# Last expert layer: gated expert rows added to token rows in DRAM tile by tile, then copied to the result

## What is computed

```python
    def _L1_ffn_ref(x, Wg, bg, W1, b1, W2, b2):
        ...
        logits = xf @ Wg.T + bg
        probs = jax.nn.softmax(logits, axis=-1)
        top2_vals, top2_idx = jax.lax.top_k(probs, 2)
        cw = jnp.zeros((n, Wg.shape[0]), dtype=x.dtype)
        cw = cw.at[jnp.arange(n)[:, None], top2_idx].set(top2_vals)
        h = jax.nn.gelu(jnp.einsum('nd,edh->neh', xf, W1) + b1[None], approximate=False)
        y = jnp.einsum('neh,ehd->ned', h, W2) + b2[None]
        out = jnp.einsum('ne,ned->nd', cw, y)
        return out.reshape(b, t, d)
    ...
    x = x + _L1_ffn_ref(_layernorm(x, axis=-1)[None], L1_ffn_Wg, L1_ffn_bg, L1_ffn_W1, L1_ffn_b1, L1_ffn_W2, L1_ffn_b2)[0]
    return x
```

## Time and profile before

| | us |
|---|---|
| median of three runs | 2013.77 (2011.37 to 2014.79) |
| the profiled execution | 2016.99 |
| its span in the profile | 2015.1 |

### The profile page before, as it was taken

One profiled execution on the slowest core, in us unless ns is written; L12 is line 12 of the kernel. 1 busy time (PEld: TensorE's weight loads), 2 busy tenths in 40 slices (PEclk: granted clock), 3 DMA queues, 4 the chain that ended last, 5 costly groups with the idle time before them and its releaser, 6 DMA issues.

```text
span 2015.1 us, 24539 instructions
## 1 busy us (share of the span) xinstructions
PE 1849.3 (92%) x8418; PEld 1165.9 (58%) x8419; DVE 746.1 (37%) x1688; ACT 401.5 (20%) x1065; POOL 128.5 (6%) x212
## 2 busy tenths in 40 slices
PE   7999999998899998599997999999999999599980
PEld 4555566566533344366666965555588589365650
DVE  3212222686688989511114311141111133311114
ACT  2431210024211222111102422000221211222110
POOL 0000000000000000111114100000000000111105
PEclk9999999999899999699998999999999999699995
DMA  6004000000000101545556111010010011545437
GB/s 183 0 1 165 3 1 0 20 1 1 14 35 33 44 28 42 196 142 185 190 185 169 55 47 47 0 47 0 1 47 1 0 55 47 203 141 182 177 117 229
DMA packets 58060, 153.06 MB, mean 76 GB/s; under 512 B 12526, under 2 KB 23170, under 8 KB 57525
## 3 DMA queue, kind: packets, MB, share of 16 engines
q1 hardware_dynamic: 34053, 87.05, 12.5%
q0 software_dynamic: 13120, 35.86, 5.9%
q10 hardware_dynamic: 10800, 28.98, 3.9%
HBM read 121.37 MB, written 33.99 MB: 77 GB/s over the span
## 4 chain that ended last, share of the span: by engine, by line
PE 81%; DVE 8%; DMA 5%; issue 2%; DVEq 2%; ACT 1%; POOL 1%; ACTq 0%; SPq 0%; POOLq 0%
PE PS L646 23%; PE PS L975 10%; PE PS L656 7%; PE PS L795 6%; PE PS L1016 4%; PE PS L1085 4%; PE PS L717 4%; PE PS L1105 4%; PE PS L1057 4%; DVE WRA L1727 3%; PE PS L1043 3%; PE PS L884 2%; DMA WS<-in_fW 2%; PE PS L893 2%; DVE WRB L1727 2%
## 5 line engine op out<-in xcount | busy, mean ns | idle before, releaser
L646 PE MATMUL PS<-WS,XT 128*125 128x384 f32 x960 | 313.3, 488 | 1.4 <-issue 1.4
L646 PEld LDWEIGHTS PS<-WS,XT 128*125 128x125 f32 x960 | 180.4, 189 | 129.3 <-issue 3.4
L975 PE MATMUL PS<-WS,XGT 128*128 x600 | 199.9, 491 | 0.0
L975 PEld LDWEIGHTS PS<-WS,XGT 128*128 128x128 f32 x600 | 113.2, 192 | 74.7 <-issue 2.5
L656 PE MATMUL PS<-XT,WS 128*128 128x416 f32 (+1 forms) x432 | 151.2, 512 | 0.0
L1727 DVE SCALAR_TENSOR_TENSOR WRA<-RB,U,AT 125x500 f32<-125x500 f32 (+1 forms) x240 | 140.1, 648 | 9.5 <-ACT AT L1205 6.8
L1856 DVE TENSOR_TENSOR YS<-PS,EBB 128x768 f32<-128x768 f32 x48 | 46.0, 958 | 256.9 <-PE PS L975 192.1
L656 PEld LDWEIGHTS PS<-XT,WS 128*128 128x128 f32 x432 | 81.6, 189 | 69.2 <-issue 69.2
L884 PE MATMUL PS<-WRA,F 125*64 125x500 f32 (+1 forms) x480 | 100.5, 537 | 10.1 <-DVE WRA L1727 9.5
L1085 PE MATMUL PS<-WS,XGT 128*128 x288 | 101.9, 505 | 7.6 <-DMA WS<-in_fW 4.9
L1105 PE MATMUL PS<-WS,HT 128*128 x276 | 94.5, 493 | 2.5 <-ACT HT L1414 2.5
(11 more groups left out here) (293 smaller groups left out, 2244.6 us busy)
## 6 DMA issues: line engine op xcount, KB each, us to landing
WS<-in_ewT SPq DMA_DIRECT2D x8, 2304.0 KB, 10.6
expert_rows<-YS ACTq DMA_DIRECT2D x48, 384.0 KB, 2.3
WS<-in_fW SPq DMA_DIRECT2D x16, 1152.0 KB, 7.5
WS<-in_w SPq DMA_DIRECT2D x5, 2304.0 KB, 10.4
xn_rows<-XN ACTq DMA_DIRECT2D x20, 336.0 KB
RB<-expert_rows SPq DMA_DIRECT2D x12, 488.3 KB
WS<-in_wp SPq DMA_DIRECT2D x2, 2304.0 KB, 11.5
WS<-in_W SPq DMA_DIRECT2D x2, 2304.0 KB, 8.1
```

Source lines behind the costliest of these rows:

```text
L646: last = nc.tensor.matmul(ps[0:T, 0:HC], lhsT[:, k, t * T:(t + 1) * T], w[:, k, b * HC:(b + 1) * HC], start=(k == 0), stop=(k == KC - 1))
L975: last = nc.tensor.matmul(PS[:, 4 + 2 * a + b, 0:HC], XGT[:, a, k, :], WS[:, bass.ds(slot, 1), k * C + b * HC:k * C + (b + 1) * HC].rearra ...
```

## The change

- While the last convolution is added (agg2_t), SP writes each finished tile of X to `expert_rows` in DRAM, at the token's own row: 20 DMAs.
- The gates are brought into tile order. DVE splits each gate into three bfloat16 parts and multiplies them into OT (TVG); PE multiplies this with OHR in 20 bfloat16 matmuls into a free PSUM bank; DVE sums the parts (GTE, the gate of each row of each tile) and forms SIDX, the DRAM row that each row of a tile belongs to. A padding row gets a row of its own behind the tokens.
- In the loop DVE multiplies YS by the gate after adding the bias (one more instruction a tile).
- ACT stores nothing any more. POOL issues, for each tile, an indirect DMA that adds the 128 rows of YS to their rows in DRAM. Each waits until the add of the tile before it has landed, as two tiles can hold the same token. POOL's index instructions are written in one stream: gather, add, gather, add.
- The 20 gathers, the 20 weighted sums and the 20 stores at the end are gone. When the last add has landed, SP and ACT copy one half each of the 1250 rows from `expert_rows` to the result, DRAM to DRAM.

POOL's inner loop of the last layer, half a turn of it, before. `turned_n30` counts tiles that PE has transposed, `ys_out30` and `ys_out31` the transfers out of the two YS buffers, `ys_ready` the tiles that DVE has scaled.

The diff, without the buffers' and semaphores' declarations and without the first layer, whose code is written out anew but does the same:

```diff
+            sp.wait_ge(dve_emptied, J.emptied("dve", J.at[f"agg2_{t}"] + 1))
+            sp.dma_start(y_d[t * T:t * T + PA, :], X[0:PA, t, :]).then_inc(acc_in, 16)
+            sp.dma_start(y_d[t * T + PA:(t + 1) * T, :], X[PA:T, t, :]).then_inc(acc_in, 16)
         sp.wait_ge(stage_done, 4)
         load(U_FF + 1)
...
-        for t in range(NT):
-            sp.wait_ge(yg_used[3], summed(3, 2 * t + 1))
-            sp.dma_start(out[t * T:t * T + PA, :], X[0:PA, t, :]).then_inc(stored, 16)
-            sp.dma_start(out[t * T + PA:(t + 1) * T, :], X[PA:T, t, :]).then_inc(stored, 16)
-        sp.wait_ge(stored, 32 * NT)
+        sp.wait_ge(y_all, 2)
+        sp.dma_start(out[0:N // 2, :].rearrange("n c -> (n c)").rearrange("(a b) -> a b", b=1920),
+                     y_d[0:N // 2, :].rearrange("n c -> (n c)").rearrange("(a b) -> a b", b=1920)).then_inc(stored, 16)
+        sp.wait_ge(stored, 32)
...
-        gathers(1, 1)
-        gathers(3, 2)
...
+        def add_rows(n, a, landed):
+
+
+            pool.wait_ge(ys_ready, n + 1)
+            for b, count in landed:
+                pool.wait_ge(ys_out[3][b], count * 16)
+            nc.gpsimd.sem_inc(pool_step, 1)
+            nc.gpsimd.tensor_tensor(SXF[:, a:a + 1], SIDX[:, bass.ds(n, 1)], ones[:, 0:1], ALU.mult)
+            pool.drain()
+            nc.gpsimd.tensor_copy(SX[:, a:a + 1], SXF[:, a:a + 1])
+            pool.drain()
+            nc.gpsimd.indirect_dma_start(out=y_d, out_offset=bass.IndirectOffsetOnAxis(ap=SX[:, a:a + 1], axis=0),
+                                         in_=YS[:, a, :], in_offset=None, compute_op=ALU.add).then_inc(ys_out[3][a], 16)
+
+        def gather3(n, a, turned):
+            pool.wait_ge(turned_n[3], turned)
+            nc.gpsimd.sem_inc(pool_step, 1)
+            gather(3, n, a)
+
+        first_gathers(3, 2)
+        n = nc.gpsimd.value_load(TAB[0:1, 2, 2:3], min_val=KT // 2 - 3, max_val=ET_MAX // 2 - 3)
+        over = nc.gpsimd.value_load(TAB[0:1, 2, 1:2], min_val=1, max_val=2)
+        for m in (2, 3, 4):
+            gather3(m, m % 2, m)
+        pool.wait_ge(gates_in, 1)
+        pool.wait_ge(acc_in, 32 * NT)
+        add_rows(0, 0, [])
+        with nc.gpsimd.Fori(0, n) as i:
+            gather3(i * 2 + 5, 1, i * 2 + 5)
+            add_rows(i * 2 + 1, 1, [(0, i + 1)])
+            gather3(i * 2 + 6, 0, i * 2 + 6)
+            add_rows(i * 2 + 2, 0, [(1, i + 1)])
+        gather3(n * 2 + 5, 1, n * 2 + 5)
+        add_rows(n * 2 + 1, 1, [(0, n + 1)])
+        gather3(n * 2 + 5, 0, n * 2 + 6)
+        add_rows(n * 2 + 2, 0, [(1, n + 1)])
+        add_rows(n * 2 + 3, 1, [(0, n + 2)])
+        with nc.gpsimd.Fori(0, over) as j:
+            add_rows(n * 2 + j + 4, 0, [(1, n + 2), (0, n + j + 2)])
+            gather3(n * 2 + j + 6, 0, n * 2 + j + 8)
+
+        pool.wait_ge(ys_out[3][0], (n + over) * 16 + 32)
+        pool.wait_ge(ys_out[3][1], n * 16 + 32)
+        nc.gpsimd.sem_inc(y_all, 1)
+        pool.wait_ge(xg_in[3][0], (n + over) * 16 + 64)
+        pool.wait_ge(xg_in[3][1], n * 16 + 48)
...
         turn(3, 1, 1, 16)
         hidden(0, 0)
+        pe.wait_ge(gate_parts, 1)
+        for q in range(KT):
+            last = nc.tensor.matmul(PS[:, 7, 0:4 * ETC], OHR[:, q, :], TVG[:, q, :, :].rearrange("p a b -> p (a b)"),
+                                    start=(q == 0), stop=(q == KT - 1))
+        last.then_inc(gates_full, 1)
         with nc.tensor.Fori(0, turns3) as i:
             for a in range(2):
...
             n = turns3 * 2 + j
             hidden_columns(n)
-            store(3, n, 0)
             columns_of(3, n + 1, 0, turned=n + 4, used=n + 2)
             gelu(n + 1, 0)
+        act.wait_ge(y_all, 2)
+        act.dma_start(out[N // 2:N, :].rearrange("n c -> (n c)").rearrange("(a b) -> a b", b=1920),
+                      y_d[N // 2:N, :].rearrange("n c -> (n c)").rearrange("(a b) -> a b", b=1920)).then_inc(stored, 16)
 
...
-            V.tensor_copy(IDXA, pos)
+            if L == 1:
+                V.tensor_copy(IDXA, pos)
             ps = full(J.at[f"tokens{L}"])
             step(V.tensor_scalar(TOKF, ps[:, 0:ETC], float(T), None, ALU.mult))
...
+            V.tensor_scalar(one(2)[:, 2:3], one(2)[:, 0:1], -2.0, None, ALU.add)
...
-            dve.wait_ge(ys_out[L][a], i * 16 + 16)
+            if L == 1:
+                dve.wait_ge(ys_out[L][a], i * 16 + 16)
+            elif not isinstance(i, int):
+                dve.wait_ge(ys_out[L][a], i * 16)
             V.tensor_tensor(YS[:, a, :].rearrange("p (b c) -> p b c", b=2), PS[:, b0:b0 + 2, 0:HC],
                             EBB[L][:, bass.ds(e, 1), :].rearrange("p a (b c) -> p (a b) c", b=2), ALU.add).then_inc(y_free[L], 1)
-
-        def weighted(L, t, n):
+            if L == 3:
+                V.drain()
+                V.tensor_scalar(YS[:, a, :], YS[:, a, :], GTE[:, bass.ds(n, 1)], None, ALU.mult).then_inc(ys_ready, 1)
...
+        V.drain()
+        V.tensor_copy(GPB[:, 0], GW)
+        V.drain()
+        V.tensor_tensor(GR, GW, GPB[:, 0], ALU.subtract)
+        V.drain()
+        V.tensor_copy(GPB[:, 1], GR)
+        V.drain()
+        V.tensor_tensor(GR, GR, GPB[:, 1], ALU.subtract)
+        V.drain()
+        V.tensor_copy(GPB[:, 2], GR)
+        V.drain()
+        tvg = TVG.rearrange("p (t k) v e -> p t k v e", k=2)
+        for n in range(2):
+            ot = OT.rearrange("p (t k) e -> p t k e", k=2)[:, :, n, :]
+            for m in range(3):
+                V.tensor_tensor(tvg[:, :, n, m, :], ot, GPB[:, m, n, :].unsqueeze(2).to_broadcast([T, NT, ETC]), ALU.mult)
+        V.tensor_copy(TVG[:, :, 3, :], OT)
+        V.drain().then_inc(gate_parts, 1)
         dve.wait_ge(eb_in, 48)
         turns3 = nc.vector.value_load(TAB[0:1, 2, 0:1], min_val=1, max_val=ET_MAX // 2 - 1)
         over3 = nc.vector.value_load(TAB[0:1, 2, 1:2], min_val=1, max_val=2)
...
-        with nc.vector.Fori(0, turns3) as i:
+        dve.wait_ge(gates_full, 1)
+        V.tensor_copy(GTE, PS[:, 7, 0:ETC])
+        V.tensor_scalar(SIDX, PS[:, 7, 3 * ETC:4 * ETC], -1.0, 1.0, ALU.mult, ALU.add)
+        V.tensor_scalar(TOKF[:, 0:1], pcol, float(N), None, ALU.add)
+        V.drain()
+        V.tensor_tensor(GTE, GTE, PS[:, 7, ETC:2 * ETC], ALU.add)
+        V.scalar_tensor_tensor(out=SIDX, in0=SIDX, scalar=TOKF[:, 0:1], in1=TOK, op0=ALU.mult, op1=ALU.add)
+        V.drain()
+        V.tensor_tensor(GTE, GTE, PS[:, 7, 2 * ETC:3 * ETC], ALU.add)
+        V.drain().then_inc(gates_in, 1)
+        for a in range(2):
+            hidden_bias(a + 1, 1 - a)
+            expert_rows(3, a, a, 0)
+        with nc.vector.Fori(1, turns3) as i:
             for a in range(2):
                 hidden_bias(i * 2 + a + 1, 1 - a)
...
-        weighted(3, 0, 0)
-        for t in range(NT):
-            if t + 1 < NT:
-                weighted(3, t + 1, 0)
-            V.drain()
-            weighted(3, t, 1)
-        V.drain().then_inc(done, 1)
```

More of the change, by code:

```diff
@@ L410, in xn_stores @@
         return 32 * (len(range(b, NT, XNB)) * (1 if L == 1 else 2))
-    def summed(L, q):
-        if L == 1:
-            return q + 1
-        return min(q + 2, KT) if q % 2 else max(q, 1)
     block_ctx = nc.Block()
@@ L592, in gathers @@
             pool.wait_ge(tab_ready, k)
-            n = nc.gpsimd.value_load(TAB[0:1, 2, 0:1], min_val=1, max_val=ET_MAX // 2 - 1)
-            over = nc.gpsimd.value_load(TAB[0:1, 2, 1:2], min_val=1, max_val=2)
-            with nc.gpsimd.Fori(0, n) as i:
-                for a in range(2):
-                    pool.wait_ge(turned_n[L], i * 2 + a + 2)
-                    gather(L, i * 2 + a + 2, a)
-            with nc.gpsimd.Fori(0, over) as j:
-                pool.wait_ge(turned_n[L], n * 2 + j * (1 if L == 1 else 2) + 2)
-                gather(L, n * 2 + j + 1, 0)
@@ L1324, in _ @@
             columns_of(1, n + 1, 0, used=n + 2)
-            store(1, n, 0)
+            store(n, 0)
         def q1_column(c, q):
@@ L1403, in _ @@
         nc.scalar.drain().then_inc(ht_ready[3], 1)
-        for b in range(2):
-            nc.scalar.drain().then_inc(ys_out[3][b], 16)
         def gelu(n, a):
@@ L1424, in _ @@
                 gelu(n + 1, 1 - a)
-                store(3, n, a)
         with nc.scalar.Fori(0, over3) as j:
```

85 lines of the change are left out of this document (52 added, 33 removed).

## The result

The changed kernel takes 2055.4 us (median of 4 runs, 2050.6 to 2060.2) and the kernel before 2012.6 in the runs beside it: a ratio of 1.021, 95% interval 1.0195 to 1.0226. It is 43 us slower. The forecast was 1981.5, and the time lies far above the range too.

What follows compares the result with a forecast made beforehand. PE was taken to bound the expert loop, leaving a 55.4 us tail to shorten. Before the loop -1.5, loads +4.3, last tile -3.6 and tail -31.5 gave -32.3 from 2013.8: 1981.5 us, range 1973 to 2002.

Steps and rivals of the forecast that it cites:

- Its period is T + 1.6: Loop, chain of adds: each issued only when the one before has landed; 6.6 us, under PE's 8.7.
- T: Loop: time of one accumulating add from issue to landing, forecast 5.0 us, ends 3.6 and 8.3.
- Per tile POOL gets 1.36 + 0.98 more ...: covered: Loop: POOL's added work per tile, beside the same for its gather, makes 4.7 of 8.7 us, so costs nothing.
- Rival (2): Slower: each row of a loop add finishes before the next, T well over 8; T=10 gives 2043 us; chance 0.14.
- Before the loop: Ahead of the expert loop: PE's gate matmuls fill a gap and the clock holds; -1.5 us, ends -2.0 and +2.4.
- Loads of weights in the loop: Four weight loads PE waits for: each add's 0.39 MB delays them 1.1, together +4.3 us, ends 0 and 16.
- The last tile: End of the loop: without ACT's store HT starts 1.7 earlier and PE's matmuls run faster; gain 3.6 us, at least 1.7.
- The tail: From the end of PE's last expert matmul to the end: 23.9 us in place of 55.4, a gain of 31.5.
- The copy: End of the tail: 3.84 MB from DRAM to DRAM lands in 14.4 us, ends 12 and 20.

Runs made afterwards that it cites:

- the control: The kernel before with the drains of the last layer's loop gathers replaced by semaphore waits; 2014.4 us, ratio 1.0006 to the kernel before.

## Why the prediction was wrong

**The step that failed** is this one: "Its period is T + 1.6, with the next gather's preparation inside T." T was forecast at 5.0 and is 5.6, so the add was hardly mis-sized, though by luck: it was summed as 3.9 for a plain transfer and 1.1 for the add's extra read, and the runs show 3.1 and 2.5. But the gather's preparation has a drain in it, and the drain ended only with T. Nor did the gather's landing lie beside anything, since the add's own preparation has a drain too. The period was T + 1.6 plus 4.8 for the gather: 12.0, where 6.6 was forecast, and above PE's 8.7. With it falls the sentence "Per tile POOL gets 1.36 + 0.98 more ...: covered". I had priced the pair by a row in which nothing of POOL's was in flight. The trace of before has the other case too, ahead of the loop, and I had read past it (POOL's timeline of the kernel before):

```profile
1744.56 0.98 POOL L582 DMA_INDIRECT XG<-xn_rows,IDX  x1 [0.79 <-PE PS L952]
1745.55 0.21 POOL L575 TENSOR_TENSOR IDXF<-TOK,ones 128x1 f32<-128x1 f32 x1
1748.61 0.18 POOL L577 CAST IDX<-IDXF 128x1 uint32<-128x1 f32 x1 [2.85 <-issue]
1749.55 0.98 POOL L582 DMA_INDIRECT XG<-xn_rows,IDX  x1 [0.77 <-issue]
...
1833.27 0.18 POOL L577 CAST IDX<-IDXF 128x1 uint32<-128x1 f32 x1 [0.22 <-issue]
```

The gather issued at 1744.56 lands 3.9 later, at 1748.5, and the cast starts at 1748.61. With the semaphores of the control the same cast came 0.17 behind its product. The last row speaks for the limits: it lies inside a load of weights that SP had issued, in flight from 1832.14 to 1842.35, and the drain cost 0.22. Of the transfers seen here it is POOL's own that count.

**Rival (2)**, slower, named the right place, the chain of adds that sets the end, and the right form, a period paid 22 times. Its price came from the wrong member: it wanted T over 8.7. Its mechanism, rows of an add finished one after the other, is not what made the period long. Its own sum with a period of 12.03 and a landing of 5.6 in it, 1764 + 22 x 12.03 + 5.6 + 15.3, gives 2049.6, and the span is 2048.8.

**The other steps** are read against the kernel without the drains, since in the changed one the loop hides them. Times are from its profiled execution, 5.0 above its own median, as that of before was 3.2 above.

| Step | Forecast | Measured |
|---|---|---|
| T, the landing of an add | 5.0 | 5.6 |
| Before the loop: from the second tile's transposes to those of its HR | -1.5 | -1.4 (19.5 to 18.1); -1.1 in the changed kernel |
| Loads of weights in the loop | +4.3 | +8.4 (189.2 to 197.6) |
| The last tile, transposes to matmuls' end | -3.6 | -3.0 (8.7 to 5.7) |
| The tail | 23.9 | 25.6 |
| The copy | 14.4 | 14.4 there, 14.7 in the changed kernel |

*Before the loop* PE's 20 gate matmuls fill the gap before tile 1's transposes, and the clock holds: the next 12 matmuls take 4.13 where they took 5.83. The timeline of PE in the changed kernel:

```profile
1746.40 1.22 PE L1166 MATMUL PS<-TVG,OHR 125*128 125x120 bf16 x20
1748.50 0.55 PE L1143 MATMUL PS<-ident,HR 128*128 128x128 f32 x3 [0.88 <-ACT HR L1461]
...
1750.05 4.13 PE L1134 MATMUL PS<-WS,XGT 128*128 x12 [0.34 <-issue]
```

All eight profiles with the gate matmuls show this 4.13. But the gain isn't certain, as the fall of the clock that it avoids doesn't come in every execution. The control has the kernel before's PE stream, with the same gap of 1.94 unfilled, and shows 4.13 as well:

```profile
1750.85 0.55 PE L1102 MATMUL PS<-ident,HR 128*128 128x128 f32 x3 [1.94 <-ACT HR L1417]
...
1752.49 4.13 PE L1093 MATMUL PS<-WS,XGT 128*128 x12 [0.44 <-issue]
```

Its stretch before the loop is 18.2, against 19.5 in the kernel before, 19.5 with two gathers and 18.1 with the change. At the last tile it is the same: behind the gap of 2.45 the 12 matmuls took 5.78 in the kernel before and 5.83 with two gathers, and 4.13 in the control. The prediction took both losses of clock from a single execution.

*The loads* are the term whose mechanism was right and whose size was off. The waits grew by 9.4 - 4.9 = 4.5, close to the 4.3. But the prediction took four equal losses, and they came as one of 3.5 and one of 2.1, while the wait for the last load, 1.2 before, was gone. Behind the gaps of 4.8 and 3.5 the clock was down, which added (6.75 - 4.13) + (5.67 - 4.13) = 4.2 more. The ends were 0 and 16, and 8.4 lies between them. It is the largest of three: by the same stretch the two later kernels with adds show +2.4 (both pairs ahead, 191.6) and +0.4 (no copy, 189.6), so the forecast of 4.3 can't be told wrong.

*The last tile*: without the store ACT's HT started early, and then the next wait took its place. Timeline of PE, kernel without drains:

```profile
1959.35 0.49 PE L1151 MATMUL PS<-ident,HR 128*128 128x128 f32 x3
1960.93 4.13 PE L1162 MATMUL PS<-WS,HT 128*128 x12 [1.08 <-DVE YS L1922]
```

The matmuls wait for DVE, which empties the PSUM tile of the one before. The gap is 1.08 and not 0.8, and behind it the clock held (4.13 and not 5.79). The rest of the 0.6 is a slip in the forecast: it took 4.13 for the matmuls behind the gap but counted the gain as 1.9, down to 3.87.

*The tail* is 1.7 longer than forecast: PE now needs only 5.7 for the last tile, less than the 7.3 from add to add, so the last add waited 4.3 for the one before it to land. In the changed kernel the tail is not even 25.6 but 33.6 from PE's end (2015.2), as two adds were still queued.

**The account** from 2013 (before) to 2055: the change as forecast -32.3, the loads with the clock +4.1, the stretch before the loop +0.1, the last tile +0.6 and the tail +1.7, which is -25.8; and the drains +68. The medians give -25.7 for the kernel without drains, but that the two meet is partly luck. The spans of the two executions from which the steps are read are only 24.4 apart, and the other 1.4 lies ahead of the second tile's transposes (1742.2 and 1743.7). It may be scatter, as the changed kernel is there at 1739.5.

What stays open: why the plain scatter waits for fewer loads than the kernel before did (0.9 to 4.9 us) although it moves the same bytes. Its gathers leave POOL 3 us later, out of some of the loads; no run separates that. Open too are why the clock falls behind the same gap in one execution and not in another, and how much of the 12.5 of the accumulation each load pays, as there is one profiled execution of each kernel.

## What to carry to other kernels

Before a step is put beside a transfer on an engine that issues transfers itself, look at what that engine does between its small instructions: a drain that cost 0.2 with nothing of its engine's in flight cost the rest of the landing behind a transfer. Replace it by a semaphore, or compute all indices ahead of all transfers, but see that the transfers don't leave later for it. When a long transfer is taken off the end, look at what ran beside it: here a closing drain of 5.06 came out from under the copy. When a gain in the tail is bought with a chain in the loop, work out the chain's period from every instruction on it, and look for a row in which its neighbours stand as they will stand.
